# A lag of 18 steps, one semaphore for two terms, and the gate o in a bank of its own, in a four-layer kernel

## The reference

```python
x = x + _L0_cond_ref(x, cond, ...)   # conditioned low-rank matrix: x + x @ layer
x = x + _L1_cond_ref(x, cond, ...)   # tanh(x @ W_ih.T + h_term)
x = x + _L2_cond_ref(x, cond, ...)   # LSTM over 2048 steps, weights Wx2, Wh2
x = x + _L3_cond_ref(x, cond, ...)   # LSTM over 2048 steps, weights Wx3, Wh3

def step(carry, xp_t):               # xp_t = x_t @ Wx + b, h0 = cond, c0 = 0
    prev_h, prev_c = carry
    h_bar = xp_t + prev_h @ Wh
    i = jax.nn.sigmoid(h_bar[:, 0:Hdim])
    f = jax.nn.sigmoid(h_bar[:, Hdim:2 * Hdim])
    o = jax.nn.sigmoid(h_bar[:, 2 * Hdim:3 * Hdim])
    g = jnp.tanh(h_bar[:, 3 * Hdim:4 * Hdim])
    next_c = f * prev_c + i * g
    next_h = o * jnp.tanh(next_c)
    return ((next_h, next_c), next_h)
```

## Time and profile before

| | us |
|---|---|
| median of 3 runs | 11900.89 (11898.32 to 11901.08) |
| the profiled execution, its time | 11900.05 |
| the profiled execution, its span | 11898.2 |
| TensorE busy | 11828.7 (99%) |
| VectorE busy | 8509.1 (72%) |
| ScalarE busy | 3758.9 (32%) |
| GpSimd busy | 1418.6 (12%) |

### The profile page before, as it was taken

One profiled execution on the slowest core, in us unless ns is written; L12 is line 12 of the kernel. 1 busy time (PEld: TensorE's weight loads), 2 busy tenths in 40 slices (PEclk: granted clock), 3 DMA queues, 4 the chain that ended last, 5 costly groups with the idle time before them and its releaser, 6 DMA issues.

```text
span 11898.2 us, 435945 instructions
## 1 busy us (share of the span) xinstructions
PE 11828.7 (99%) x231604; PEld 2698.0 (23%) x100532; DVE 8509.1 (72%) x46342; ACT 3758.9 (32%) x24698; POOL 1418.6 (12%) x5238
## 2 busy tenths in 40 slices
PE   8999999999999999999999999999999999999999
PEld 5222222222222222222222222222222222222222
DVE  2677777777777777777777777777777777777776
ACT  2233333333333333333333333333333333333332
POOL 4011111111111111111111111111111111111110
PEclk9999999999999999999999999999999999999999
DMA  4000000000000000000000000000000000000000
GB/s 164 25 4 5 4 5 4 5 5 4 5 5 4 5 5 4 5 4 5 4 5 5 4 5 5 4 5 5 4 5 4 5 4 5 5 4 5 5 5 3
DMA packets 374546, 107.86 MB, mean 9 GB/s; under 512 B 349594, under 2 KB 357830, under 8 KB 372436
## 3 DMA queue, kind: packets, MB, share of 16 engines
q1 hardware_dynamic: 362372, 61.96, 2.8%
q0 software_dynamic: 3504, 11.56, 0.3%
q10 hardware_dynamic: 6560, 6.32, 0.2%
HBM read 62.98 MB, written 16.78 MB: 7 GB/s over the span
## 4 chain that ended last, share of the span: by engine, by line
PE 99%; DVE 0%; issue 0%; ACT 0%; POOLq 0%; POOL 0%; DVEq 0%
PE bank L80 89%; PE bank L874 7%; PE bank L518 1%; PE bank L531 1%; PE bank L484 0%; DVE gates_t L1055 0%; DVE gates_t L1062 0%; ACT gate_o L950 0%; DVE state L1085 0%; DVE state L1088 0%; DVE state L1081 0%; ACT tanh_c L952 0%; DVE pre L1068 0%; DVE pre L1061 0%; DVE g_fc L1065 0%
## 5 line engine op out<-in xcount | busy, mean ns | idle before, releaser
L80 PE MATMUL bank<-wh,state 128*6 128x512 bf16 x196608 | 11055.6, 379 | 20.8 <-DVE state L1088 20.8
L1054 DVE STREAM_TRANSPOSE gates_t<-bank 128x256 f32<-128x256 f32 x4096 | 1843.6, 450 | 2015.3 <-PE bank L80 2013.7
L80 PEld LDWEIGHTS bank<-wh,state 128*6 128x6 bf16 x65536 | 1568.1, 86 | 7400.5 <-issue 6498.0
L945 ACT ACTIVATE gate_if<-pre 128x8 f32<-128x8 f32 x4096 | 859.8, 210 | 7256.0 <-DVE pre L1059 7256.0
L1081 DVE TENSOR_TENSOR state<-gate_o,tanh_c 128x8 f32<-128x8 f32 x4096 | 688.2, 168 | 836.0 <-ACT tanh_c L952 811.2
L1062 DVE STREAM_TRANSPOSE gates_t<-bank 128x128 f32<-128x128 f32 x4096 | 1252.5, 306 | 0.0
L1055 DVE STREAM_TRANSPOSE gates_t<-bank 128x128 f32<-128x128 f32 x4096 | 1122.9, 274 | 0.0
L983 POOL TENSOR_TENSOR y<-x,state 128x8 f32<-128x8 f32 x2048 | 434.5, 212 | 5374.2 <-DVE state L1088 5374.2
L950 ACT ACTIVATE gate_o<-pre 128x8 f32<-128x8 f32 x4096 | 855.0, 209 | 642.8 <-DVE pre L1068 642.4
L983 POOL TENSOR_TENSOR x<-x1r,state 128x8 f32<-128x8 f32 x2048 | 434.5, 212 | 4961.2 <-DVE state L1088 4961.2
L952 ACT ACTIVATE tanh_c<-g_c 128x8 f32<-128x8 f32 x4096 | 854.7, 209 | 9.7 <-DVE g_c L1072 9.7
(11 more groups left out here) (124 smaller groups left out, 3490.6 us busy)
## 6 DMA issues: line engine op xcount, KB each, us to landing
w<-in_w SPq DMA_DIRECT2D x8, 2048.0 KB, 13.2
out<-y_rows SPq DMA_DIRECT2D x1020, 8.0 KB, 1.8
wx<-in_x SPq DMA_DIRECT2D x16, 512.0 KB, 5.4
x1p<-x_t_all SPq DMA_DIRECT2D x128, 64.0 KB, 2.6
x1r<-x_t_all SPq DMA_DIRECT2D x128, 64.0 KB, 2.6
x_t_all<-wx ACTq DMA_DIRECT2D x6, 1024.0 KB, 4.8
wx<-in_Wh POOLq DMA_DIRECT2D x8, 512.0 KB, 4.2
wx<-in_Wh POOLq DMA_DIRECT2D x16, 256.0 KB, 4.9
```

The costliest lines, as they stand in the source:

```text
L80: return pe.add_instruction(mybir.InstMatmult(name=nc.get_next_instruction_name(), engine=mybir.EngineType.PE, ins=[pe.lower_ap(moving), p ...
L945: act.activation(gate_if[l][:, 1, :, 1], pre[l][:, HB:2 * HB], ACT.Sigmoid).then_inc(S[l]["f"], 1)
L1054: dve.transpose(gates_t[l][:, 0:gf, NS * NB:], banked[:, 0:gf]).then_inc(s["trans_if"], 1)
```

## The change

There are four parts. The lag becomes 18, and the step of `ROWS_AT` follows from it (3 instead of 4). The semaphores g (raised by ScalarE's tanh of g) and fc (raised by VectorE's product of f and c) become one, terms, raised by both; since it counts two per step, the others that VectorE waits for count two per step too (`BOTH`). In the lone steps of the fourth layer at the end, TensorE sums i, f and g first (48 matmuls of 384 columns into bank10) and then o (48 of 128 columns into bank00, the third layer's, which is free by then), with a semaphore mm_o of its own, for which VectorE's transpose of o waits. With a lag of 18 the fourth layer's last chunk begins in step 2 of chunk 128, which needs all four quarters before; so in step 1 of chunk 128 VectorE turns quarters 2 and 3 as well, which are projected in that same step, and GpSimd takes the bias adds of that step ahead of the residual.

```diff
-LAG = CH + 2 + 1
+LAG = CH + 2
...
+        found = [x[:3] for x in found if x[3] == NH - 1]
+        if self.number == NCH:
+
+            own = [(L3, -1, 2), (L3, -1, 3)]
+            found = [x for x in found if x not in own] + (own if s == 1 else [])
+        return found
+
+    def lone(self):
+
+        return self.number is not None and self.number >= NCH
+
+    def own_turned(self, s):
+
+        return self.number == NCH and s == 1
...
-                def matmuls(l):
-
-                    w = wh[l][:, :, :, :, :, :, :].rearrange("p h k j s m c -> p h k j s (m c)")
+                def matmuls(l, to=None, first=0, last=NMS):
+
+                    to = gates[l][:, 0:NMS * C] if to is None else to
+                    w = wh[l][:, :, :, :, :, first:last, :].rearrange("p h k j s m c -> p h k j s (m c)")
...
-                            matmuls(l).then_inc(S[l]["mm"], 1)
+                            if t.lone():
+
+                                ifg = 3 * NH // NS
+                                matmuls(l, gates[l][:, 0:ifg * C], 0, ifg).then_inc(S[l]["mm"], BOTH)
+                                matmuls(l, gates[L2][:, 0:NMS * C - ifg * C], ifg).then_inc(S[l]["mm_o"], 1)
+                            else:
+                                matmuls(l).then_inc(S[l]["mm"], BOTH)
...
-                            act.activation(g_fc[l][:, :, 0], pre[l][:, 2 * HB:3 * HB], ACT.Tanh).then_inc(S[l]["g"], 1)
+                            act.activation(g_fc[l][:, :, 0], pre[l][:, 2 * HB:3 * HB], ACT.Tanh).then_inc(S[l]["terms"], 1)
...
+                            if t.own_turned(s):
+                                for x in t.done_before(l, s):
+                                    add_bias(x[0], t, *x[1:])
+                                residual(l, t, s)
+                            else:
+                                residual(l, t, s)
+                                for x in t.done_before(l, s):
+                                    add_bias(x[0], t, *x[1:])
...
+                            apart = banked[:, ifg:]
+                            if t.lone():
+                                apart = gates[L2][:, 0:NMS * C - ifg * C].rearrange("p (m c) -> p m c", c=C)
+                                dve.wait_ge(s["mm_o"], t.count(l, step) - NCH * CH + LAG)
+                            dve.transpose(gates_t[l][:, ifg:, NS * NB:], apart).then_inc(s["trans_o"], BOTH)
 
                             dve.wait_ge(s["f"], n)
                             dve.tensor_tensor(g_fc[l][:, :, 1], gate_if[l][:, 1, :, 1], g_c[l][:, :, 1],
-                                              ALU.mult).then_inc(s["fc"], 1)
+                                              ALU.mult).then_inc(s["terms"], 1)
...
-                            dve.wait_ge(s["fc"], n)
-                            dve.wait_ge(s["g"], n)
+                            dve.wait_ge(s["terms"], n)
```

42 lines of the change are left out of this document (19 added, 23 removed).

## The result

The changed kernel takes **12056.34 us** (median of 4 runs, 12055.14 to 12061.86) against 11900.74 before (4 runs, 11898.32 to 11901.08): a ratio of 1.0132, 95% interval 1.0116 to 1.0148. It is 1.3% slower, far outside the range of 11879 to 11894. The profiled execution took 12057.39 us, its span is 12055.6.

What follows compares the result with a forecast made beforehand. It took TensorE as the bound in the middle, and matmuls plus exposed chain in lone steps. Terms -4.8 - 1.6 - 11.5 + 1.0 = -16.9 us led to 11884.0 us, range 11879 to 11894.

Steps and rivals of the forecast that it cites:

- What bounds the kernel: Whole span: TensorE 99% busy, no wait to win in the middle; lone steps are matmuls plus chain, 2.59 + 2.59 us.
- (a): Lag of 18: one lone layer-4 step fewer at the end, -5.19 us, front +0.39; sum -4.8.
- (d): Second lone step: VectorE also turns quarters projected in that same step, so the state comes later, +1.0 us.
- The readiness priced at 0: Each chunk's first layer-4 step: input terms come in time, with 0.43 us of slack; cost 0 for 126 chunks.
- rival 2: Each chunk's first layer-4 step: input terms late through ScalarE's wait for GpSimd; 11931 us at 0.8 late; chance 5%.
- (b): Scan waits on one semaphore, starting 0.07 us earlier in 23 exposed chains: -1.6 us; in the pairs 0.
- (c): Lone steps at the end: o summed apart lets the chain start 0.64 us earlier, 18 steps, -11.5 us.
- The slower one: The same as rival 2: late input terms in each chunk's first layer-4 step, 11931 us at 0.8 late; chance 5%.
- The 3% kept for the unknown: Whole kernel: 3% chance of a gain above 0.2% by something not seen.
- rival 4: Clock drop after gaps near the first lone steps: 1.65 us lower without it, 1.65 higher with another; no chance given.

Runs made afterwards that it cites:

- the semaphores alone: Changed kernel with lag 19 and o not split, so only its semaphore part against the kernel before: 12040.96 us, ratio 1.0118.

## Why the prediction was wrong, point by point

**What bounds the kernel.** The views were read rightly for the kernel before: no wait of TensorE in the middle. The step that failed is the sentence after that, that no wait can be *won* there and so nothing there needs a price. It asks only for gain. The prediction had the numbers for the loss: two sets of matmuls at 2.59 and a unit at 0.22 make a plain pair of 5.40, and a layer's circle is 5.19. So 0.21 us stood between some 1500 plain pairs and a bound by the chain, and it was not written down. Slack was worked out at one place only, a chunk's first layer-4 step (0.43).

**(a) The lag.** Right in itself. At the end -5.19 and (d) together came to -3.93 instead of -4.2, at the front +0.48 instead of +0.39. The readiness priced at 0 is 0 with quick hand-overs (steps 2 and 3 at 5.617). In the changed kernel it is not: the bias add, ScalarE's copy and the reduction are each behind a slower hand-over.

```profile
5046.37 0.47 POOL L1014 TENSOR_TENSOR area<-turned,bias_all 128x128 f32<-128x128 f32 x1
...
5046.92 0.22 ACT L963 COPY gates_t<-area 128x32 f32<-128x32 f32 x1 [1.60 <-POOL area L1014]
...
5047.24 0.22 DVE L1086 TENSOR_REDUCE pre<-gates_t 128x16 f32<-128x64 f32 x1 [0.25 <-ACT gates_t L963]
```

The copy starts 0.08 behind the add where the row used had 0.03, and the reduction waits 0.25 in this row, 0.28 on the average of 124 chunks, on a chain that is itself 0.25 longer. So a part of rival 2 came true after all, in company: steps 2 and 3 are 0.076 and 0.120 longer than before, and the 124 chunks of the changed kernel take 31.8 us more than those of the semaphores alone, at 19.

**(b) One semaphore.** This is the step that failed, twice. "In the pairs it shortens a hidden chain: 0" prices the one wait that goes and not the other half of the edit, that every semaphore VectorE waits for counts by two. The diff names it (`BOTH`), the order of instructions showed the same rows with and without it, and I took an add of two for as cheap as an add of one. It costs a layer's chain 0.25 us net (five sites of 0.06 to 0.07, less some 0.05 won at the scan, which starts 0.12 behind the reduction of o where it was 0.165). Over 0.21 of slack that is 0.05 per plain pair, and with the late starts and steps 2 and 3 it makes +159 us in 124 chunks. Also the part that was right was too small: in the run with counts by one, the semaphore wins 0.06 per lone step (4.49 against 4.552) and 5.5 us in the pairs, where the prediction had 0, since the scan's split-off wait goes and with it most of its late starts.

The Trainium skill (VectorE: DVE Perf Modes, "The DRAIN you can't avoid") reports that a semaphore raised after each of eight copies cost nothing extra. No run here takes a semaphore away by itself. Adds of two in place of one on instructions without a wait fit it (11904.05 against 11900.02, not told apart from no change); an instruction that also waits and adds two is another case, at 0.06 to 0.07 us.

**(c) The split of o.** Right to the hundredth: 0.056 per pack of 128 columns, 0.67 for o, a transpose that doesn't wait, 0.64 a step. In the changed kernel the steps are 4.80 apart, because 4.55 gets the same 0.25 as every other chain.

**(d)** measured 1.2 instead of 1.0.

**The rivals.** None of the four names the mechanism. The slower one had the right kind (a hand-over that exceeds its slack once in every chunk), but asked only whether one added wait was late, by a hand-over time taken from before. The 3% kept for the unknown stood on the side of a gain. The clock (rival 4) did what its bounds say: the drop after the gap ahead of the first lone step is absent in the changed kernel (2.62 us from its first matmul to the next group, at 11960.75 after a gap of 2.68) and present in the ten kernels of the experiments, up to 1.7 us.

```profile
11960.75 2.79 PE L80 MATMUL bank<-wh,state 128*6 128x384 bf16 x96 [2.68 <-DVE state L1118]
11963.37 1.92 PE L890 MATMUL bank<-wx,x 128*32 128x128 f32 x64
```

**The sum.** With the semaphores taken out, -16.9 + 1.6 = -15.3 stands against 11887.13 - 11900.97 = -13.8; with the scan's semaphore in and counts by one, -16.9 against 11880.31 - 11900.02 = -19.7. The second pair is close partly by luck: without the 5.5 us in the pairs, which the sum had at 0, it would be -14.2. So the terms that were priced hold within 3 us, and one that was not seen is ten times their sum.

## What to carry to other kernels

Before calling an engine's middle safe, write down the slack of every chain that is hidden in it (here 0.21 us in a pair of 5.40), and price every edit that touches each step against that slack, also one that seems only to renumber. Semaphores that are raised by instructions which themselves wait should count by one; where one semaphore needs two raisers, let each add one and give its wait a value of its own, as in the run of 11880.31 us. And a TensorE that is 99% busy can hide 120 us of waiting, since waits shorter than a matmul's record minus its pitch don't show as idle: compare the distances between starts.

## What the runs showed of the hardware that I had not expected

- An instruction carries its wait and an add of one together, but a wait and an add of two are issued as two instructions, 0.062 us apart on ScalarE and 0.066 on VectorE. A second wait of an instruction is issued apart too: the scan starts 0.10 behind the reduction with one wait, 0.165 with two.
- Behind a wait that is issued alone one start in 100 to 180 is some 0.29 (ScalarE) to 0.36 us (VectorE) late, at the same places of the loop's body in every pass, a multiple of 128 records of the engine's stream apart. That points at the supply of instructions, but no run here varies it, so the cause stays open.
- Packs of four 128-column bf16 matmuls with different column tiles start 0.056 us apart, 0.014 per matmul, over 12 packs.
